# Remainder products straight from the gathered rows, two casts of ScalarE in another order, and GpSimd's lookups ahead of its first-layer product

## The chip, the cores and the metric

The kernel runs on one core of a Trainium2 chip. The metric is the device time of one execution in microseconds (us), median of three runs. Engines are called TensorE (PE in the rows), VectorE (DVE), ScalarE (ACT), GpSimd (POOL) and SyncE (SP, whose DMA queue is SPq).

## The reference

For each of 1024 samples, 32 ids look up 32 rows of 64 numbers, one in each of 32 tables. These rows are h0 (32 fields, 64 columns). Two "cross" layers follow, each a product of every pair of fields, column by column, mixed by a weight, with a bias and a relu; then a sum over the 64 columns and a small perceptron.

```
def _cin_layer(h, h0, W, b):
    Wr = W.reshape(W.shape[0], Hn, Mn)
    x = jnp.einsum('bhd,bmd,ohm->bod', h, h0, Wr) + b[None, :, None]
    return jax.nn.relu(x)
e = jnp.stack([tbl_0[ids[:, 0]], ..., tbl_31[ids[:, 31]]], axis=1)
x1 = _cin_layer(e, e, W1, b1)              # 128 outputs
x2 = _cin_layer(x1[:, :64], e, W2, b2)     # 128 outputs
z = sum over columns of concat(x1[:, 64:], x2)
h = relu(concat(z, dense_ctx) @ W_top1 + b_top1)
h = relu(h @ W_top2 + b_top2)
y = h @ W_top3
```

All is float32.

## The kernel before

**Tiling.** A chunk is 8 samples, so 8 x 64 = 512 columns; there are 128 chunks and 64 pairs of chunks. The looked-up rows of a pair come by four indirect DMAs of GpSimd (the lookups, L271) into one of three buffers `gathered`, 128 partitions (32 fields x 4) by 4 x 64 numbers. They are stored twice to a table in DRAM, `emb_rows` (L234), laid out by field. From there each chunk is loaded in several forms: `h0` (every field four times), `near` (four tiles, fields shifted by 0 to 15) and `far` (four tiles, fields shifted by 16 to 31).

**First layer.** The product of a pair of fields is symmetric, so only shifts 0 to 16 are needed. Shifts 0 to 15 are `prod1 = near * h0` (one instruction of GpSimd a chunk, L308), then eight matmuls in plain float32 (L592: four tiles, two instructions each). The shift by 16 has only 16 distinct products, field f by field f + 16: this is the remainder. Before, it is loaded from DRAM a pair of chunks at a time as `rem_a` (fields 0 to 15) and `rem_b` (fields 16 to 31), each 32 rows of 512 (L352); GpSimd multiplies them into `rem_prod` (L279), ScalarE casts the product twice to the rounded type fp32r, into two blocks of `rem_parts` (L727, L728), and GpSimd writes what the rounding lost into the third block (L295). One matmul of 96 rows (L595) adds the three blocks to the accumulator `acc1` and ends it.

**Second layer.** ScalarE takes relu and sums of `acc1` (L713, writes `x1`), SyncE replicates rows of `x1` by DMA (L251, `x1rep`), ScalarE copies that into PSUM (L762, `x1p`), and VectorE multiplies it with `near` and with `far` (L514, `pnear` and `pfar`, eight tiles each). Ten near and far tiles and three more, 13 in all, are split into a rounded part `phi` and the rest `plo`, and multiplied with rounded weights `w2hi` and `w2lo` in fp32r: two matmuls on `phi` (L604, L605) and one on `plo` (L610) for each tile. Two of these 13 tiles get their `plo` from a DMA that adds (L285, 512 KB, issued by GpSimd, in `low_parts`); the other 11 from VectorE (L519). The remaining three tiles go in plain float32 (L615, six instructions). ScalarE makes `phi` by three casts: near tiles 2 to 7 (L789), near tiles 0 and 1 (L790) and five far tiles (L801), and then takes relu and sums of the second layer's accumulator of the chunk before (L713 again, named acc<-acc).

**Order.** Each engine runs one hand-written program; they meet only in semaphores. After a fill, every engine has a function `step(c, ...)`, run for chunk c = 0 to 127. In step c TensorE does, in this order: the 12 `phi` matmuls of near tiles 2 to 7, the four of near tiles 0 and 1, the whole first layer of chunk c + 2 (L592, L595), then L615, L610 and the ten `phi` matmuls of the far tiles. ScalarE's step c begins with relu and sums of the first layer of chunk c + 1. SyncE's step c waits for these (`z1_ready`), replicates `x1`, loads `h0` and `near` of chunk c + 3, in even steps stores a pair's rows, loads `far` of chunk c + 2, and in even steps loads the remainder of the pair. GpSimd's step c does `prod1` of chunk c + 2, the adding DMA, in odd steps the remainder's product, in even steps its low part, and last two lookups; the lookups of an even step come behind a small copy of four columns of indices (L266).

TensorE's clock has two levels, 1.2 and 2.4 GHz; PEclk in the profile is the granted share of the higher.

Of the kernel before, what the change touches and what calls it, by code (L numbers as in the profile page):

```python
# [42 lines left out]
def build_dlrm(nc, a):  # L43
# [7 lines left out]
    with ctx:  # L51
# [15 lines left out]
        idx = [sb(f"idx_{s}", [P, PAIR_GATHERS], i32) for s in range(3)]  # L67
# [15 lines left out]
        rem_a = sb("rem_a", [REM, N])  # L83
        rem_b = sb("rem_b", [REM, N])
        rem_prod = sb("rem_prod", [REM, N])
        rem_parts = sb("rem_parts", [3 * REM, N], fp32r)
# [44 lines left out]
        idx_ready = sem("idx_ready")  # L131
# [20 lines left out]
        x1p_ready = sem("x1p_ready")  # L152
        rem_in = sem("rem_in")
# [101 lines left out]
        @block.gpsimd  # L255
        def _(pool):
            nc.gpsimd.memset(ident[:, :], 0.0).then_inc(ident_zero, 1)
            pool.wait_ge(ident_zero, 1)
            nc.gpsimd.affine_select(out=ident[:, :], in_=ident[:, :], compare_op=ALU.not_equal, fill=1.0,
                                    base=0, pattern=[[-1, P]], channel_multiplier=1).then_inc(ident_ready, 1)  # L260
            nc.gpsimd.memset(wt1a[0:H, :], 0.0)
            nc.gpsimd.memset(z1[0:H, :], 0.0).then_inc(top_zero, 1)
            pool.wait_ge(idx_all_ready, 1)

            def place_idx(pair, s):
                nc.gpsimd.tensor_copy(idx[s][:, :].unsqueeze(2), idx_all[:, :, bass.ds(pair, 1)]).then_inc(idx_ready, 1)  # L266
                pool.wait_ge(idx_ready, pair + 1)
                pool.sem_inc(lookups_begun, 1)

            def gather(g, s):  # L270
                nc.gpsimd.indirect_dma_start(  # L271
                    out=gathered[s][:, g, :], out_offset=None, in_=a["tables"],
                    in_offset=bass.IndirectOffsetOnAxis(ap=idx[s][:, g:g + 1], axis=0)).then_inc(rows_gathered[s], 16)

            def remainder_products(pair):
                pool.wait_ge(rem_in, 32 * pair + 32)

                pool.wait_ge(rem_lo_ready, pair)
                nc.gpsimd.tensor_tensor(rem_prod[:, :], rem_a[:, :], rem_b[:, :], ALU.mult).then_inc(rem_prod_ready, 1)  # L279

            def low_parts(c):

                pool.wait_ge(minus_ready, c + 1)
                pool.sem_inc(lo_begun, 1)
                nc.gpsimd.dma_start(plo[:, 0:T_DMA, :], pnear[:, 0, 0:T_DMA, :], accum_op=ALU.add  # L285
                                    ).then_inc(lo_dma_in, 16)

            for pair in range(3):
                place_idx(pair, pair)
                for g in range(PAIR_GATHERS):  # L290
                    gather(g, pair)

            def remainder_low(pair):
                pool.wait_ge(rem_hi_ready, pair + 1)
                nc.gpsimd.tensor_tensor(rem_parts[2 * REM:3 * REM, :], rem_prod[:, :],  # L295
                                        rem_parts[0:REM, :].bitcast(fp32), ALU.subtract).then_inc(rem_lo_ready, 1)

            def step(c, turn, u, at):
                pair, odd = turn * (U // 2) + u // 2, u % 2
                if at == 0:  # L300
                    pool.wait_ge(rem_prod_ready, 2)
                    remainder_low(1)
                    pool.wait_ge(rem_lo_ready, 2)
                if within(at, 2):

                    pool.wait_ge(acc1_ready, c + 2)
                    pool.wait_ge(near_in[(u + 2) % 3], LOADS * (turn * (U // 3)) + LOADS * ((u + 2) // 3 + 1))
                    nc.gpsimd.tensor_tensor(prod1[:, :, :], near[(u + 2) % 3][:, :, :],  # L308
                                            h0[odd][:, :].unsqueeze(1).to_broadcast([P, K1, N]), ALU.mult
                                            ).then_inc(p1_ready, 1)  # L310
# [3 lines left out]
                if not odd and begun(at) and within(at, 2):  # L314

                    pool.wait_ge(p1_ready, c + 3)
                    remainder_low(pair + 1)
                    pool.wait_ge(rem_lo_ready, pair + 2)
                if within(at, 7 - odd):
                    if not odd:  # L320
                        if at == 0:
                            pool.wait_ge(p1_ready, 3)

                        pool.wait_ge(emb_stored, STORES * pair + STORES)
                        place_idx(pair + 3, u // 2)
                    for g in range(2 * odd, 2 * odd + 2):
                        gather(g, u // 2)

            remainder_products(1)
            all_steps(step)  # L330

        @block.sync
        def _(sp):
# [28 lines left out]
            store_copy(sp, 0, 0, 0)  # L362
            sp.wait_ge(emb_stored, STORES)
            load_h0(sp, 0, 0, 0)
            load_near_tiles(sp, 0, 0, range(0, K1 // 2))
            load_rem(0)
            load_near(sp, N, 1, 1)
            store_rows(1, 1, 1)
            load_far(0, 0)
            sp.wait_ge(emb_stored, 2 * STORES)  # L370
            sp.wait_ge(rem_prod_ready, 1)
            load_rem(2 * N)
            sp.wait_ge(z1_ready, 1)
            replicate_x1(sp, [0])

# [18 lines left out]
            def step(c, turn, u, at):  # L394
# [17 lines left out]
                if not odd and within(at, 5):  # L412

                    sp.wait_ge(emb_stored, STORES * pair + 3 * STORES)
                    sp.sem_inc(stores_begun, 1)
                    sp.wait_ge(rem_prod_ready, pair + 2)
                    load_rem((c + 4) * N)
# [10 lines left out]
        def _(dve):  # L428
# [10 lines left out]
            dve.wait_ge(idx_ready, 2)  # L439
# [48 lines left out]
            def products1(s, ks):  # L488
# [7 lines left out]
            dve.wait_ge(rem_in, 32)  # L496
            nc.vector.tensor_tensor(rem_prod[:, :], rem_a[:, :], rem_b[:, :], ALU.mult).then_inc(rem_prod_ready, 1)
# [4 lines left out]
            dve.wait_ge(rem_hi_ready, 1)  # L502
            nc.vector.tensor_tensor(rem_parts[2 * REM:3 * REM, :], rem_prod[:, :],
                                    rem_parts[0:REM, :].bitcast(fp32), ALU.subtract).then_inc(rem_lo_ready, 1)
# [16 lines left out]
            def step(c, turn, u, at):  # L521
# [3 lines left out]
                if begun(at):  # L525
                    dve.wait_ge(lo_near_ready, c)
                    dve.wait_ge(lo_dma_in, 16 * c)
# [22 lines left out]
        def _(pe):  # L550
# [43 lines left out]
            def remainder1(s):  # L594
                nc.tensor.matmul(acc1[s][:, :], w1remT[:, s, :], rem_parts[:, :],  # L595
                                 start=False, stop=True).then_inc(acc1_ready, 1)

            def layer1(s):
                tiles1(s, range(K1))
                remainder1(s)  # L600
# [22 lines left out]
            pe.wait_ge(rem_lo_ready, 1)  # L623
            remainder1(0)
# [3 lines left out]
            layer1(1)  # L628
# [6 lines left out]
            def step(c, turn, u, at):  # L635
# [5 lines left out]
                pe.wait_ge(hi_dma_ready, c + 1)  # L641
                high(odd, range(0, T_DMA)).then_inc(hi_near_used, 1)
                if within(at, 2):
                    pe.wait_ge(p1_ready, c + 3)
                    pe.wait_ge(rem_lo_ready, pair + 2)
                    pe.wait_ge(z1_ready, c + 1)
                    layer1(odd)
# [5 lines left out]
                else:  # L653
# [7 lines left out]
                    top1(3)  # L661
                pe.wait_ge(pfar_ready, c + 1)
# [45 lines left out]
        def _(act):  # L708
# [16 lines left out]
            def remainder_hi(pair):  # L725
                act.wait_ge(rem_prod_ready, pair + 1)
                nc.scalar.copy(rem_parts[0:REM, :], rem_prod[:, :])  # L727
                nc.scalar.copy(rem_parts[REM:2 * REM, :], rem_prod[:, :]).then_inc(rem_hi_ready, 1)  # L728
# [15 lines left out]
            load_near_tiles(nc.scalar, 0, 0, range(K1 // 2, K1))  # L744
            act.wait_ge(w2_second, 1)
# [6 lines left out]
            remainder_hi(0)  # L752
# [20 lines left out]
            def step(c, turn, u, at):  # L773
# [6 lines left out]
                if not odd and within(at, 2):  # L780
                    remainder_hi(pair + 1)
# [8 lines left out]
                nc.scalar.copy(phi[:, 0:T_DMA, :], products[:, 0:T_DMA, :]).then_inc(hi_dma_ready, 1)  # L790
# [7 lines left out]
                act.wait_ge(pfar_ready, c + 1)  # L798
                if begun(at):
                    act.wait_ge(acc2_ready, c)  # L800
                nc.scalar.copy(phi[:, T_NEAR:T_SPLIT, :], pfar[:, :, :, :].rearrange("p a k n -> p (a k) n")[:, 0:T_SPLIT - T_NEAR, :]).then_inc(hi_far_ready, 1)  # L801
# [38 lines left out]
```

## Time and profile before

| what | value |
|---|---|
| median of three runs | 2034.03 us (2031.25 to 2035.14) |
| the profiled execution, its own time | 2035.26 us |
| span of the profile | 2033.5 us, mean granted clock 0.997 |
| TensorE busy | 1999.9 us (98%) |
| VectorE busy | 1923.5 us (95%) |
| ScalarE busy | 1713.6 us (84%) |
| GpSimd busy | 1647.3 us (81%) |
| DMA share of 16 engines, 100 to 1900 us | 0.90 to 0.91 |

Busy shares are means over the span. What sets the end is read from who waits for whom: an engine that never waits is the bound, and idle time of another costs nothing until that first one has to wait for it. Overlap of matmuls is modelled, so the distance from the start of one to the start of the next is the cost of a matmul in a stream, not its own duration.

### The profile page before, as it was taken

How to read it: one execution, taken by the hardware profiler on the slowest of the kernel's cores; microseconds unless marked ns; L12 is line 12 of the kernel's file. 1: busy time of each engine (PE TensorE's matmuls, PEld its weight loads, DVE VectorE, ACT ScalarE, POOL GpSimd, SP SyncE). 2: the span in 40 equal slices, each digit the busy share in tenths (PEclk: the TensorE clock that was granted, in tenths of full speed). 3: DMA queues.
4: the chain of work that ended last, by engine and by line, in shares of the span. 5: the costliest groups of instructions: out<-in, count | busy, mean ns of one | idle time of the engine just before them, and what ended most of it. 6: DMA issues, size and time to landing. Idle time of an engine off the chain costs nothing.

```text
span 2033.5 us, 24093 instructions
## 1 busy us (share of the span) xinstructions
PE 1999.9 (98%) x7038; PEld 1325.8 (65%) x7038; DVE 1923.5 (95%) x546; ACT 1713.6 (84%) x4887; POOL 1647.3 (81%) x708
## 2 busy tenths in 40 slices
PE   5999999999999999999999999999999999999999
PEld 3666666666666666666666666666666666666664
DVE  6999999999999999999999999999999999999991
ACT  4788888888888888888888888888888888888873
POOL 5898887879899998887889998788999988887520
PEclk9999999999999999999999999999999999999999
DMA  7898988988988989989989989989988989989950
GB/s 227 217 268 235 245 246 232 245 248 232 245 249 234 248 244 235 250 241 236 253 237 237 254 237 236 257 232 237 257 233 238 255 231 239 255 230 238 251 131 11
DMA packets 257782, 474.16 MB, mean 233 GB/s; under 512 B 35425, under 2 KB 52321, under 8 KB 257522
## 3 DMA queue, kind: packets, MB, share of 16 engines
q1 hardware_dynamic: 230450, 396.18, 64.5%
q0 software_dynamic: 26624, 75.52, 22.0%
q8 instruction: 56, 0.92, 0.2%
q10 hardware_dynamic: 576, 0.92, 0.1%
q14 instruction: 76, 0.62, 0.1%
HBM read 321.49 MB, written 16.78 MB: 166 GB/s over the span
## 4 chain that ended last, share of the span: by engine, by line
PE 90%; DMA 3%; DVE 2%; ACT 2%; issue 2%; POOL 1%; SPq 0%; DVEq 0%; POOLq 0%; ACTq 0%
PE acc L592 20%; PE acc L604 17%; PE acc L605 17%; PE acc L610 17%; PE acc L615 14%; DMA plo<-pnear 2%; DVE pnear L514 2%; PE acc L595 1%; ACT phi L789 1%; ACT x L713 1%; POOL prod L308 1%; DMA x1rep<-x 1%; PE x1p L686 0%; DMA near<-emb_rows 0%; PE acc L686 0%
## 5 line engine op out<-in xcount | busy, mean ns | idle before, releaser
L271 POOL DMA_INDIRECT gathered<-in_tables,idx x256 | 655.4, 2560 | 101.8 <-POOL idx L266 51.2
L308 POOL TENSOR_TENSOR prod<-near,h 128x2048 f32<-128x2048 f32 x126 | 582.5, 4623 | 128.5 <-PE acc L595 81.1
L604 PE MATMUL acc<-phi,w2lo 128*128 128x512 f32 x1664 | 655.2, 394 | 8.2 <-ACT phi L789 8.0
L605 PE MATMUL acc<-phi,w2hi 128*128 128x512 f32 x1664 | 654.3, 393 | 0.0
L514 DVE TENSOR_TENSOR pnear<-near,x1p 128x4096 f32<-128x4096 f32 x128 | 564.9, 4413 | 6.2 <-ACT x1p L762 3.8
L514 DVE TENSOR_TENSOR pfar<-far,x1p 128x4096 f32<-128x4096 f32 x128 | 564.9, 4413 | 0.7 <-PE acc L615 0.7
L592 PE MATMUL acc<-prod,w1T 128*128 128x512 f32 x1024 | 460.1, 592 | 1.5 <-DVE prod L489 1.5
L610 PE MATMUL acc<-plo,w2hi 128*128 128x512 f32 x1664 | 454.5, 423 | 0.0
L713 ACT ACTIVATE x<-acc,bias 128x64 f32<-128x64 f32 x1024 | 305.8, 324 | 170.6 <-PE acc L595 170.6
L519 DVE TENSOR_TENSOR plo<-pnear,phi 128x3072 fp32r<-128x3072 f32 x128 | 446.2, 3486 | 0.3 <-ACT phi L789 0.3
L519 DVE TENSOR_TENSOR plo<-pfar,phi 128x2560 fp32r<-128x2560 f32 x128 | 361.2, 2822 | 45.1 <-ACT phi L801 45.0
L610 PEld LDWEIGHTS acc<-plo,w2hi 128*128 128x128 f32 x1664 | 313.0, 188 | 120.6 <-issue 61.0
L604 PEld LDWEIGHTS acc<-phi,w2lo 128*128 128x128 f32 x1664 | 314.1, 189 | 82.3 <-ACT phi L789 12.8
L605 PEld LDWEIGHTS acc<-phi,w2hi 128*128 128x128 f32 x1664 | 314.1, 189 | 67.9
L789 ACT CAST phi<-pnear 128x3072 fp32r<-128x3072 f32 x128 | 352.7, 2756 | 0.0
L615 PE MATMUL acc<-pfar,w2T 128*128 128x512 f32 x768 | 350.6, 592 | 0.0
L592 PEld LDWEIGHTS acc<-prod,w1T 128*128 128x128 f32 x1024 | 193.6, 189 | 197.0 <-issue 184.5
L801 ACT CAST phi<-pfar 128x2560 fp32r<-128x2560 f32 x128 | 299.5, 2340 | 0.0
L713 ACT ACTIVATE acc<-acc,bias 128x64 f32<-128x64 f32 x1024 | 293.5, 291 | 4.8 <-PE acc L605 4.8
L615 PEld LDWEIGHTS acc<-pfar,w2T 128*128 128x128 f32 x768 | 145.7, 190 | 159.3 <-issue 153.7
L713 ACT ACTIVATION_READ_ACCUMULATOR x<-acc,bias 128x1 f32 x1024 | 220.9, 216 | 0.0
L713 ACT ACTIVATION_READ_ACCUMULATOR acc<-acc,bias 128x1 f32 x1024 | 218.1, 213 | 0.0
(75 smaller groups left out, 1151.3 us busy)
## 6 DMA issues: line engine op xcount, KB each, us to landing
far<-emb_rows SPq DMA_DIRECT2D x512, 256.0 KB, 4.6
near<-emb_rows SPq DMA_DIRECT2D x510, 256.0 KB
plo<-pnear POOLq DMA_DIRECT2D x128, 512.0 KB
x1rep<-x SPq DMA_DIRECT2D x255, 256.0 KB, 4.3
h<-emb_rows SPq DMA_DIRECT2D x128, 256.0 KB
emb_rows<-gathered SPq DMA_DIRECT2D x127, 128.0 KB
gathered<-in_tables,idx POOLq DMA_INDIRECT x256, 6.6
rem_a<-emb_rows SPq DMA_DIRECT2D x64, 64.0 KB
```

Of the source, the lines that this page charges most:

```text
L271: nc.gpsimd.indirect_dma_start(out=gathered[s][:, g, :], out_offset=None, in_=a["tables"], in_offset=bass.IndirectOffsetOnAxis(ap=idx[s][: ...
L308: nc.gpsimd.tensor_tensor(prod1[:, :, :], near[(u + 2) % 3][:, :, :], h0[odd][:, :].unsqueeze(1).to_broadcast([P, K1, N]), ALU.mult).then_ ...
L514: return nc.vector.tensor_tensor(out, h0part.unsqueeze(1).to_broadcast([P, A2, k, N]), x1p[s][:, :].rearrange("p (a n) -> p a n", a=A2).un ...
L519: return nc.vector.tensor_tensor(plo[:, parts, :], whole, phi[:, parts, :].bitcast(fp32), ALU.subtract)
L592: nc.tensor.matmul(acc1[s][:, :], w1T[:, k, :], prod1[:, k, :], start=(k == 0), stop=False)
L604: nc.tensor.matmul(acc2[s][:, :], w2lo[:, t, :], phi[:, t, :], start=(t == T_DMA), stop=False)
L605: mm = nc.tensor.matmul(acc2[s][:, :], w2hi[:, t, :], phi[:, t, :], start=False, stop=(t == T_SPLIT - 1))
L610: mm = nc.tensor.matmul(acc2[s][:, :], w2hi[:, t, :], plo[:, t, :], start=False, stop=False)
L615: mm = nc.tensor.matmul(acc2[s][:, :], w2T[:, k, :], pfar[:, 1, K2 - T_WHOLE + k, :], start=False, stop=False)
L713: ins = nc.scalar.activation(out[:, cols], acc[:, cols], ACT.Relu, bias=bias[:, :], accum_out=z[:, bass.ds(c * CB + b, 1)])
L789: nc.scalar.copy(phi[:, T_DMA:T_NEAR, :], products[:, T_DMA:T_NEAR, :]).then_inc(hi_near_ready, 1)
L801: nc.scalar.copy(phi[:, T_NEAR:T_SPLIT, :], pfar[:, :, :, :].rearrange("p a k n -> p (a k) n")[:, 0:T_SPLIT - T_NEAR, :]).then_inc(hi_far_ ...
```

## The change

**Remainder.** `rem_a` and the two loads from DRAM go. For each pair SyncE now moves partitions 64 to 127 of `gathered` (fields 16 to 31) to `rem_b` on partitions 0 to 63 (`move_upper`, one DMA of 64 KB), GpSimd multiplies `gathered[0:64]` with it (64 x 256 in place of 32 x 512), ScalarE makes one cast (`rem_hi`), GpSimd the low part (`rem_lo`), and SyncE places the three blocks into one of two buffers `rem_parts` by three DMAs of 64 KB (`place_remainder`). TensorE waits for these DMAs (`rem_in`, 48 a pair) ahead of the first layer, where it had waited for GpSimd's low part.

**ScalarE.** The far cast comes ahead of the copy into `x1p`, and the cast of near tiles 0 and 1 behind both. The remainder's cast moves to the end of odd steps, ahead of the second layer's relu and sums. TensorE runs the four `phi` matmuls of near tiles 0 and 1 behind the first layer, no longer ahead of it.

**GpSimd.** In each step the two lookups come first, ahead of `prod1`, and read their indices from `idx_all` directly; the copy L266 goes. The low part of the remainder comes at the head of even steps.

```diff
             def step(c, turn, u, at):        # GpSimd
                 pair, odd = turn * (U // 2) + u // 2, u % 2
-                if at == 0:
-                    pool.wait_ge(rem_prod_ready, 2)
-                    remainder_low(1)
-                    pool.wait_ge(rem_lo_ready, 2)
+                if not odd and begun(at) and within(at, 2):
+                    remainder_low(pair + 1)
+                if within(at, 7 - odd):
+                    if not odd:
+                        pool.wait_ge(emb_stored, STORES * pair + STORES)
+                        pool.wait_ge(rem_prod_ready, pair + 1)
+                    for g in range(2 * odd, 2 * odd + 2):
+                        gather(g, pair + 3, u // 2)
                 if within(at, 2):
                     pool.wait_ge(acc1_ready, c + 2)
...
                 low_parts(c)
                 if odd and within(at, 3):
-                    remainder_products(pair + 2)
...
+                    remainder_products(pair + 2, (u // 2 + 2) % 3)
...
-            def load_rem(col):
-
-                for t, f0 in ((rem_a, 0), (rem_b, HALF)):
-                    src = bass.AP(emb, f0 * ROW + col, [[ROW, HALF], [N, 2], [1, N]])
-                    sp.dma_start(t[:, :], src).then_inc(rem_in, 16)
+            def move_upper(pair, s):
+
+                if pair:
+                    sp.wait_ge(rem_prod_ready, pair)
+                sp.dma_start(rem_b[:, :, :], gathered[s][HALF * GS:F * GS, :, :]).then_inc(rem_b_in, 16)
+
+            def place_remainder(pair):
+
+                sp.wait_ge(rem_lo_ready, pair + 1)
+                if pair >= 2:
+                    sp.wait_ge(acc1_ready, 2 * pair - 2)
+                for b, part in enumerate((rem_hi, rem_hi, rem_lo)):
+                    home = rem_parts[pair % 2][b * REM:(b + 1) * REM, :].rearrange("r (w n) -> r w n", w=2)
+                    sp.dma_start(home.bitcast(fp32), part[:, :].bitcast(fp32)).then_inc(rem_in, 16)
...
                     sp.wait_ge(pnear_ready, c + 1)
                     sp.wait_ge(p1_ready, c + 2)
+                    if odd:
+                        sp.wait_ge(emb_stored, STORES * (pair + 3))
                     load_near(sp, (c + 3) * N, 1 - odd, u % 3)
+                if not odd and begun(at) and within(at, 2):
+                    place_remainder(pair + 1)
                 if not odd and within(at, 5):
                     store_rows(pair + 2, (u // 2 + 2) % 3, turn + (u // 2 + 2) // 3 + 1)
+                    move_upper(pair + 2, (u // 2 + 2) % 3)
...
                 high(odd, range(T_DMA, T_NEAR))
-                pe.wait_ge(hi_dma_ready, c + 1)
-                high(odd, range(0, T_DMA)).then_inc(hi_near_used, 1)
                 if within(at, 2):
                     pe.wait_ge(p1_ready, c + 3)
-                    pe.wait_ge(rem_lo_ready, pair + 2)
+                    pe.wait_ge(rem_in, 48 * (pair + 2))
                     pe.wait_ge(z1_ready, c + 1)
-                    layer1(odd)
+                    layer1(odd, pair + 1)
...
+                pe.wait_ge(hi_dma_ready, c + 1)
+                high(odd, range(0, T_DMA)).then_inc(hi_near_used, 1)
```

In the fill, the first remainder's product moves from VectorE to GpSimd, behind its twelve lookups, and the first layer of chunk 0 waits for its three placing DMAs.

## Rows read from the trace of the kernel before

**Rows 1.** Waits of TensorE, 100 to 1900 us: total us, times, longest

```profile
PE acc L604 <- ACT phi L789: 1.5, 3, 0.5
```

**Rows 2.** Chain that ended last, 1000 to 1034 us: start us, us

```profile
1009.53 0.23 PE acc L604
...
1012.28 0.23 PE acc L604
...
1013.20 3.43 PE acc L592 x8
...
1028.38 3.43 PE acc L592 x8
```

**Rows 3.** Timeline of ScalarE: start us, us, [idle before <- releaser]

```profile
1008.84 1.04 ACT L790 CAST phi<-pnear 128x1024 fp32r<-128x1024 f32 x1
...
1009.79 1.00 ACT L762 COPY x1p<-x1rep 128x1024 f32<-128x1024 f32 x1
...
1010.73 2.34 ACT L801 CAST phi<-pfar 128x2560 fp32r<-128x2560 f32 x1
...
1012.98 0.27 ACT L713 ACTIVATE acc<-acc,bias 128x64 f32<-128x64 f32 x1
...
1016.90 0.31 ACT L713 ACTIVATE x<-acc,bias 128x64 f32<-128x64 f32 x1 [1.47 <-PE acc L595]
...
1019.24 0.60 ACT L727 CAST rem_parts<-rem_prod 32x512 fp32r<-32x512 f32 x1
```

**Rows 4.** Timeline of SyncE's DMA queue in two even steps: issue start us, us

```profile
928.35 1.20 SPq L251 DMA_DIRECT2D x1rep<-x  x2
...
936.62 1.24 SPq L234 DMA_DIRECT2D emb_rows<-gathered  x2
...
1019.47 1.20 SPq L251 DMA_DIRECT2D x1rep<-x  x2
...
1026.56 2.57 SPq L234 DMA_DIRECT2D emb_rows<-gathered  x2
```

**Rows 5.** Timeline: a near load's issue, and the product that waits for it

```profile
900.53 5.55 SPq L242 DMA_DIRECT2D near<-emb_rows  x4
...
910.89 4.61 POOL L308 TENSOR_TENSOR prod<-near,h 128x2048 f32<-128x2048 f32 x1 [0.31 <-DMA near<-emb_rows]
```

**Rows 6.** Landing times of line L251's x1rep and L346's far loads

```profile
DMA to landing us min/median/max: 3.6/4.4/6.0
...
DMA to landing us min/median/max: 3.2/4.6/7.3
```

**Rows 7.** Timeline of TensorE behind two of its idle stretches

```profile
64.70 0.50 PE L604 MATMUL acc<-phi,w2lo 128*128 128x512 f32 x1 [2.29 <-ACT phi L789]
...
70.08 3.59 PE L592 MATMUL acc<-prod,w1T 128*128 128x512 f32 x8
...
1984.47 0.79 PE L604 MATMUL acc<-phi,w2lo 128*128 128x512 f32 x1 [4.18 <-ACT phi L789]
...
1991.05 1.02 PE L574 MATMUL acc<-z,wt1a 128*128 128x512 f32 x2
```

**Rows 8.** Busy time by window: PE PEld DVE ACT POOL, PEclk, DMA, GB/s

```profile
1986.00:1989.00 3.00, 3.00 (x9) 2.32 (x8) 3.00 (x2) 1.60 (x1) 0.00 (x0) 0.50 0.12 22
```

**Rows 9.** The page's row of the lookups: busy, mean ns, idle

```profile
L271 POOL DMA_INDIRECT gathered<-in_tables,idx x256 | 655.4, 2560 | 101.8 <-POOL idx L266 51.2
```

**Rows 10.** Chain that ended last, 0 to 100 us: the adding DMA

```profile
48.16 8.21 DMA plo<-pnear
```

**Rows 11.** Timeline of VectorE and GpSimd in steady state

```profile
1015.88 4.41 DVE L514 TENSOR_TENSOR pnear<-near,x1p 128x4096 f32<-128x4096 f32 x1
...
1022.91 0.99 POOL L285 DMA_DIRECT2D plo<-pnear  x1
```

**Rows 12.** Timeline of the fill: GpSimd's last lookup, TensorE's first remainder

```profile
25.38 1.42 POOL L271 DMA_INDIRECT gathered<-in_tables,idx  x1 [0.30 <-issue]
...
28.89 0.80 PE L595 MATMUL acc<-rem_parts,w1remT 96*128 96x512 f32 x1
```

More of the change, by code:

```diff
@@ L66, in build_dlrm @@
         idx_all = sb("idx_all", [P, PAIR_GATHERS, PAIRS], i32)
-        idx = [sb(f"idx_{s}", [P, PAIR_GATHERS], i32) for s in range(3)]
         gathered = [sb(f"gathered_{s}", [P, PAIR_GATHERS, D]) for s in range(3)]
@@ L82, in build_dlrm @@
         far = [sb(f"far_{s}", [P, K2, N]) for s in range(2)]
[L83 to L86, printed above, removed]
+        rem_b = sb("rem_b", [HALF * GS, PAIR_GATHERS, D])
+        rem_prod = sb("rem_prod", [HALF * GS, PAIR_GATHERS * D])
+        rem_hi = sb("rem_hi", [HALF * GS, PAIR_GATHERS * D], fp32r)
+        rem_lo = sb("rem_lo", [HALF * GS, PAIR_GATHERS * D], fp32r)
+        rem_parts = [sb(f"rem_parts_{s}", [3 * REM, N], fp32r) for s in range(2)]
         prod1 = sb("prod1", [P, K1, N])
@@ L152, in build_dlrm @@
         x1p_ready = sem("x1p_ready")
+        rem_b_in = sem("rem_b_in")
         rem_in = sem("rem_in")
@@ L312, in step @@
                 if odd and within(at, 3):
-                    remainder_products(pair + 2)
[L314 to L329, printed above, removed]
+                    remainder_products(pair + 2, (u // 2 + 2) % 3)
+            for pair in range(2):
+                remainder_products(pair, pair)
+                remainder_low(pair)
             all_steps(step)
@@ L362, in _ @@
             store_copy(sp, 0, 0, 0)
+            move_upper(0, 0)
             sp.wait_ge(emb_stored, STORES)
@@ L365, in _ @@
             load_near_tiles(sp, 0, 0, range(0, K1 // 2))
-            load_rem(0)
             load_near(sp, N, 1, 1)
             store_rows(1, 1, 1)
+            move_upper(1, 1)
+            place_remainder(0)
             load_far(0, 0)
             sp.wait_ge(emb_stored, 2 * STORES)
-            sp.wait_ge(rem_prod_ready, 1)
-            load_rem(2 * N)
             sp.wait_ge(z1_ready, 1)
             replicate_x1(sp, [0])
+            place_remainder(1)
             sp.wait_ge(tp_copied, 2)
@@ L411, in step @@
                     load_far((c + 2) * N, odd)
[L412 to L417, printed above, removed]
                 if at == 3:
@@ L592, in tiles1, with remainder1, layer1 @@
                     nc.tensor.matmul(acc1[s][:, :], w1T[:, k, :], prod1[:, k, :], start=(k == 0), stop=False)
-            def remainder1(s):
-                nc.tensor.matmul(acc1[s][:, :], w1remT[:, s, :], rem_parts[:, :],
+            def remainder1(s, pair):
+                nc.tensor.matmul(acc1[s][:, :], w1remT[:, s, :], rem_parts[pair % 2][:, :],
                                  start=False, stop=True).then_inc(acc1_ready, 1)
-            def layer1(s):
+            def layer1(s, pair):
                 tiles1(s, range(K1))
-                remainder1(s)
+                remainder1(s, pair)
             def high(s, parts):
@@ L622, in _ @@
             tiles1(0, range(K1 // 2, K1))
-            pe.wait_ge(rem_lo_ready, 1)
-            remainder1(0)
+            pe.wait_ge(rem_in, 48)
+            remainder1(0, 0)
             turn(6, *NEAR_TURNS[1])
@@ L726, in remainder_hi @@
                 act.wait_ge(rem_prod_ready, pair + 1)
-                nc.scalar.copy(rem_parts[0:REM, :], rem_prod[:, :])
-                nc.scalar.copy(rem_parts[REM:2 * REM, :], rem_prod[:, :]).then_inc(rem_hi_ready, 1)
+                if pair:
+                    act.wait_ge(rem_in, 48 * pair)
+                nc.scalar.copy(rem_hi[:, :], rem_prod[:, :]).then_inc(rem_hi_ready, 1)
             act.wait_ge(ident_ready, 1)
@@ L779, in step @@
                     layer1(c + 1, 1 - odd)
-                if not odd and within(at, 2):
-                    remainder_hi(pair + 1)
                 act.wait_ge(pnear_ready, c + 1)
@@ L789, in step @@
                 nc.scalar.copy(phi[:, T_DMA:T_NEAR, :], products[:, T_DMA:T_NEAR, :]).then_inc(hi_near_ready, 1)
-                nc.scalar.copy(phi[:, 0:T_DMA, :], products[:, 0:T_DMA, :]).then_inc(hi_dma_ready, 1)
+                act.wait_ge(pfar_ready, c + 1)
+                if begun(at):
+                    act.wait_ge(acc2_ready, c)
+                nc.scalar.copy(phi[:, T_NEAR:T_SPLIT, :], pfar[:, :, :, :].rearrange("p a k n -> p (a k) n")[:, 0:T_SPLIT - T_NEAR, :]).then_inc(hi_far_ready, 1)
                 if within(at, 1):
@@ L797, in step @@
                     copy_x1rep(1 - odd)
[L798 to L801, printed above, removed]
+                nc.scalar.copy(phi[:, 0:T_DMA, :], products[:, 0:T_DMA, :]).then_inc(hi_dma_ready, 1)
+                if odd and within(at, 3):
+                    remainder_hi(pair + 2)
                 if at == CHUNKS - 1:
```

40 lines of the change are left out of this document (17 added, 23 removed).

## The prediction

> **What bounds the kernel now.** I read the page first, but busy shares don't decide here: four engines are above 80%. The view that decides is TensorE's list of waits. From 100 to 1900 us it waited 1.5 us in all [rows 1]. The chain that ended last says the same: step after step it is TensorE's matmuls end to end, and the first layer of one chunk starts 15.18 us behind that of the chunk before [rows 2]. So the steady part is 15.2 us of matmuls a step and no wait. The change leaves every matmul in place. It can win nothing there; it can win in the fill and the drain, which are few, or it can lose wherever something that TensorE waits for now comes too late. The reader should therefore ask of each edit only this: when is it ready, and when does TensorE want it?
>
> I count from s, the start of TensorE's step c with c odd, 1009.53 in the rows. In the kernel before the first layer begins at s + 3.67, behind sixteen phi matmuls; the thirteenth of them starts at 1012.28, s + 2.75 [rows 2]. Its end shows in ScalarE, which waited for it and began relu and sums at 1016.90, s + 7.37 [rows 3]; SyncE could replicate x1 at 1019.47, 2.57 us later [rows 3, 4]. That is the even step's SyncE program, and the change adds to it.
>
> **The remainder's new way (the term that decides).** In even steps SyncE places the pair's three blocks behind its near load, and TensorE wants them ahead of the first layer of the same even step. Before, this had a step of slack: the loads were SyncE's last work and the low part was GpSimd's. Now both ends lie in one step, so I add up the way between.
>
> - The first layer now stands behind twelve matmuls, so the wanted time in the even step is s + 15.18 + 2.75 = s + 17.93, and the odd step's first layer ends at s + 2.75 + 3.66 = s + 6.4 (3.43 and a remainder of 0.23).
> - ScalarE begins its far cast at s at the earliest, since it needs the accumulation that ends there. By distances from start to start: far cast 2.25, copy into x1p 0.94, near cast 0.95 [rows 3]. The remainder's cast of 64 x 256 does half the columns of one that took 0.60 [rows 3]; I take 0.3, with nothing and 0.6 as ends. Then relu and sums of the second layer; eight pairs like it, from the row of 1016.90 to the cast behind them at 1019.24, take 2.3 [rows 3]. Sum 6.8, so ScalarE is free at about s + 6.9, past s + 6.4. The relu of the first layer starts there, 0.5 us sooner than before.
> - SyncE's replication: + 2.57, at s + 9.5.
> - From the replication to the end of the near load (where the stores now start): 1019.47 to 1026.56 is 7.1 us, 928.35 to 936.62 is 8.3 [rows 4]. I take 7.9: place_remainder begins at s + 17.4 (16.6 to 17.8). It is already about the time at which TensorE wants the data.
> - Three DMAs; one issue costs 0.6 by the pair of replications (1.20 for two) [rows 4], so the third starts 1.25 us on, at s + 18.6.
> - Landing. No row shows 64 KB behind a near load. The nearest are 256 KB ones: 4.4 in the median and 3.6 at least for x1rep, which copies inside SBUF too, 4.6 (3.2 to 7.3) for far [rows 6]. The last near load itself landed at 910.89, 4.8 us behind the end of its issue at 906.08 [rows 5]. I take 4.4, the same kind of copy; ends 3.2 and 7.3. Landed at s + 23.0 (21.0 to 26.4).
>
> TensorE waits from s + 17.93 to s + 23.0: **5.1 us a pair** (3.1 to 8.5). By the Trainium skill (DMA: Bandwidth & Descriptors, Anatomy of one DMA) one DMA costs about 2.0 us and its bytes by 436 GB/s, 2.15 us for 64 KB; the wait would be 2.8 us by that, an estimate by that page. The rows here have 3.6 at the least for 256 KB, where that rule gives 2.6, so I stay with the rows.
>
> **The clock behind the wait.** After 2.29 us idle the sixteen phi matmuls took from 64.70 to 70.08, 5.4 us, and after 4.18 us idle from 1984.47 to 1991.05, 6.6 us [rows 7]; in steady state they take 3.67 [rows 2]. The granted clock behind the second was 0.50 [rows 8], the lower of the two levels. So an idle stretch costs another 1.7 to 2.9 us. Mine is 5.1 long: I take 2.8, ends 0 and 3.
>
> The odd step gets nothing back, because TensorE is full of its own work from there. The relation of every other engine eases (VectorE's 1923.5 us over 128 steps is 15.0 a step, against a mean of 19). A pair costs 7.9 us more. Places happen in even steps 2 to 124, 62 of them: 62 x 7.9 = 490 us.
>
> **ScalarE's order.** What VectorE waits for the far cast goes when the far cast comes first. It is worth nothing, since TensorE waits for nobody. The near cast of tiles 0 and 1 ends at s + 4.1, wanted behind the first layer at s + 6.4: hidden. If that cover were gone, its 0.95 would fall on TensorE. The copy into x1p is 1.3 us later than before, at s + 2.3 to 3.3; VectorE wants it at s + 6.35 (1015.88) [rows 11]: hidden. TensorE frees near tiles 0 and 1 3.7 us later, at s + 7.3; ScalarE touches them again behind 10 us: hidden.
>
> **GpSimd's order.** Dropping L266 frees one copy and its idle, 0.8 us each (51.2 us in all) [rows 9]. Against that the low part now waits for ScalarE's cast at the end of the odd step, s + 4.5, and with it the two lookups, prod1 and the adding DMA queued behind. Low part 0.7 (half of a 32 x 512 one's work; estimate from the 0.60 cast, ends 0.3 and 1.3), lookups 2 x 2.56 and 0.3 of issue each, prod1 4.6 [rows 5, 9]: prod1 ends at s + 15.6, wanted at s + 17.93: hidden. The adding DMA starts at s + 15.6; before it was s + 13.4 (1022.91) [rows 11]. Landed 8.2 us later [rows 10], at s + 23.8, where VectorE wanted to overwrite pnear at about 1015.88 + 15.18, s + 21.5. That 2.3 us lie inside the wait above. If that wait is not there, this one is (a rival below).
>
> **Fill.** The first remainder was done at 28.89 [rows 12]. Now GpSimd starts it behind twelve lookups, which ended at 26.80 [rows 12], about 24 without the copies. Product 0.7, cast 0.3, low part 0.7, issue 1.85, landing 4.4: about 32. I count 4 us of loss (0 to 8). Two or three moves of 64 KB more a pair are below 3% of the DMA's bytes: 0.
>
> **Sum.** 2035.3 (the profiled execution's own time, 1.2 us over the median of the runs) + 490 + 4 = 2529. The slower pace leaves the DMA engines emptier, so near loads are issued nearer to 7.1 than 7.9; that takes off about 0.3 a pair, 19 us. I forecast **2510 us**.
>
> **Rivals.**
> A. The wait is there but shorter: near issue 7.1, landing 3.2, 3.1 us a pair, and with a clock loss of 1.7 it is 4.8 x 62: 2035 + 298 = 2333; with no fall of the clock 2230. For: emptier DMA engines. Against: rows 7 show the fall after 2.29 us.
> B. The blocks land in time, by a shorter issue than any row has. Then the adding DMA decides: 2.3 late, less the 0.7 that ScalarE's phi now has in hand (pnear 4.4 and casts 3.8 from s + 21.5 end at s + 29.7, wanted at s + 30.4): 1.6 x 62, 2134 us. It decides once the place is under s + 18.
> C. Much longer: landing 7.3 behind near's backlog, 8.5 + 3 a pair, 2035 + 713 = 2750.
> D. Faster: everything lands in time and TensorE stays full. Then only the fill counts: three index copies of about 1 us less, and of the idle in [rows 7] 2.29 us: some 5 us, 2030. Its point is a landing before s + 17.93, so a place of three DMAs within 0.5 us of its begin. No row is near. The same edits with the fill's loss against them give no change, 2034.
>
> **How the numbers follow.** Forecast (2400 to 2650) 0.60; A 0.20; B 0.08; C 0.05; D 0.04; no change 0.03. The range leaves out most of B, D and the top of C: 2220 to 2670. A run of this kernel repeats within about 0.2%, so that is the bound of no change. Faster 0.04, same 0.03, slower 0.93.
>
> **What would show it.** The list of waits of TensorE must have L592 behind the DMA of rem_parts, about 62 times, 4 to 6 us each; granted clock about 0.5 for some 5 us behind each; SyncE's three placing issues about 17 us behind s; VectorE and GpSimd's shares down to about 77% and 66%. If TensorE's waits name phi or plo, B is right. I would be wrong if SyncE got through its near load in 4 us, or if the data were wanted a step later than I read the counts.

## The result and the profile after

The changed kernel takes 2500.86 us (median of four runs, 2497.16 to 2508.85) against 2034.34 us. The ratio is 1.230, 95% interval 1.227 to 1.234: slower by 467 us, or 7.52 us for each of the 62 pairs of chunks that are placed in the loop. The forecast was 2510 us.

The page of the changed kernel, span, engines, clock and DMA share:

```profile
span 2507.0 us, 24032 instructions
...
PE 2134.1 (85%) x7038; PEld 1366.7 (55%) x7038; DVE 1916.3 (76%) x544; ACT 1663.8 (66%) x4823; POOL 1223.2 (49%) x646
...
PEclk9989999899889889899999898899999899999999
DMA  7777678778777677687787787777777777777760
```

No engine has more work that would explain it: VectorE, ScalarE and GpSimd are all busy for less time than before. The list of waits of TensorE, 100 to 2400 us, is what answers to [rows 1]:

```profile
PE acc L591 <- issue: 329.6, 60, 6.6
```

There was one reason to wait in the steady part, worth 1.5 us; now there is another, ahead of the first layer (L591), once a pair, 5.5 us each. Over the whole execution it is 339.8 us in 62 waits. The profile can't name the releaser here and says "issue". TensorE waits for three things in that place: prod1, the blocks (`rem_in`) and x1's relu (`z1_ready`). Which of them it is, the experiments must tell. The page's row of these matmuls shows the second part of the loss:

```profile
L591 PE MATMUL acc<-prod,w1T 128*128 128x512 f32 x1024 | 587.2, 727 | 341.3 <-issue 339.8
```

The same 1024 matmuls were busy for 460.1 us before (592 ns each). So 127.1 us went into their being slower. 339.8 + 127.1 = 466.9 of the 473.5 us between the two spans. The other 6.6 us are a sum of small parts: TensorE starts the remainder matmul of chunk 3 3.2 us later than before (76.31 against 73.11), the drain behind the last one is 3.5 us shorter (69.8 against 73.3), and some 7 us lie in the steady part, outside these two rows.

The chain that ended last, over one pair (answers to [rows 2]):

```profile
1028.03 0.23 PE acc L603
...
1030.77 3.43 PE acc L591 x8
...
1045.97 5.19 issue
1051.17 5.88 PE acc L591 x8
```

An odd step c starts at s = 1028.03. Its first layer takes 3.43 us at once. In the even step behind it the first layer was due at 1045.97 and starts 5.19 us later, and then takes 5.88 us for the same eight matmuls. One pair earlier the wait was 6.57 us, up to 1012.64, and the eight took 6.37 us. The windows around that earlier first layer (columns as in [rows 8]) show the clock at the lower level, and back at 0.99 in the third window:

```profile
1012.00:1015.00 3.00, 2.36 (x3) 1.18 (x4) 2.17 (x1) 0.00 (x0) 0.00 (x0) 0.50 0.92 293
1015.00:1018.00 3.00, 3.00 (x5) 1.12 (x4) 0.00 (x0) 0.00 (x0) 0.00 (x0) 0.50 0.03 12
1018.00:1021.00 3.00, 3.00 (x11) 1.82 (x10) 0.00 (x0) 1.72 (x12) 1.67 (x1) 0.99 0.00 0
```

What TensorE waited for stands in the timeline of SyncE's queue in the same even step (answers to [rows 4]):

```profile
1037.43 1.20 SPq L253 DMA_DIRECT2D x1rep<-x  x2
1038.73 1.15 SPq L239 DMA_DIRECT2D h<-emb_rows  x1
1039.92 4.63 SPq L244 DMA_DIRECT2D near<-emb_rows  x4
1044.65 2.48 SPq L354 DMA_DIRECT2D rem_parts<-rem_hi  x2
1047.17 0.61 SPq L354 DMA_DIRECT2D rem_parts<-rem_lo  x1
```

The first placing DMA is issued 1.3 us ahead of the time at which TensorE wants all three landed, and the third 1.2 us behind it.

### The profile page after: what moved, and what is told of

It is laid out like the page before. It is cut to its first block, busy times and chain, and to the rows that moved or that the text cites. A ratio compares the mean times of both kernels' runs of the same rounds, so it can differ in the third digit from the quotient of the medians.

```text
span 2507.0 us, 24032 instructions
## 1 busy us (share of the span) xinstructions
PE 2134.1 (85%) x7038; PEld 1366.7 (55%) x7038; DVE 1916.3 (76%) x544; ACT 1663.8 (66%) x4823; POOL 1223.2 (49%) x646
## 4 chain that ended last, share of the span: by engine, by line
PE 83%; issue 14%; DVE 1%; DMA 0%; ACT 0%; SPq 0%; POOL 0%; DVEq 0%; POOLq 0%; ACTq 0%
PE acc L591 23%; PE acc L603 15%; PE acc L604 15%; PE acc L609 15%; PE acc L614 13%; PE acc L594 1%; DVE pnear L512 0%; DMA plo<-pnear 0%; PE x1p L685 0%; PE acc L685 0%; ACT phi L789 0%; DVE plo L517 0%; DMA near<-emb_rows 0%; POOL prod L313 0%; PE x1p L562 0%
## 5 line engine op out<-in xcount | busy, mean ns | idle before, releaser
L512 DVE TENSOR_TENSOR pfar<-far,x1p 128x4096 f32<-128x4096 f32 x128 | 565.9, 4421 | 509.7 <-PE acc L614 509.7
L591 PE MATMUL acc<-prod,w1T 128*128 128x512 f32 x1024 | 587.2, 727 | 341.3 <-issue 339.8
L512 DVE TENSOR_TENSOR pnear<-near,x1p 128x4096 f32<-128x4096 f32 x128 | 565.4, 4417 | 19.4 <-DMA plo<-pnear 13.9
L591 PEld LDWEIGHTS acc<-prod,w1T 128*128 128x128 f32 x1024 | 236.3, 238 | 629.5 <-issue 622.5
L517 DVE TENSOR_TENSOR plo<-pnear,phi 128x3072 fp32r<-128x3072 f32 x128 | 431.9, 3374 | 0.0
L268 POOL DMA_INDIRECT gathered<-in_tables,idx_all x256 | 392.3, 1532 | 71.5 <-issue 66.2
L517 DVE TENSOR_TENSOR plo<-pfar,phi 128x2560 fp32r<-128x2560 f32 x128 | 361.5, 2824 | 0.0
L712 ACT ACTIVATE acc<-acc,bias 128x64 f32<-128x64 f32 x1024 | 287.5, 284 | 5.7 <-PE acc L604 5.7
L788 ACT ACTIVATE plo<-pnear 128x1024 fp32r<-128x1024 f32 x128 | 136.1, 1063 | 184.3 <-PE acc L609 171.4
L295 POOL TENSOR_TENSOR rem_lo<-rem_prod,rem_hi 64x256 fp32r<-64x256 f32 x64 | 75.6, 1181 | 369.2 <-ACT rem_hi L729 368.7
L712 ACT ACTIVATION_READ_ACCUMULATOR x<-acc,bias 128x1 f32 x1024 | 228.5, 223 | 0.0
```

Of the source, the lines that this page charges most:

```text
L268: nc.gpsimd.indirect_dma_start(out=gathered[s][:, g, :], out_offset=None, in_=a["tables"], in_offset=bass.IndirectOffsetOnAxis(ap=idx_all[ ...
L512: return nc.vector.tensor_tensor(out, h0part.unsqueeze(1).to_broadcast([P, A2, k, N]), x1p[s][:, :].rearrange("p (a n) -> p a n", a=A2).un ...
L517: return nc.vector.tensor_tensor(plo[:, parts, :], whole, phi[:, parts, :].bitcast(fp32), ALU.subtract)
L591: nc.tensor.matmul(acc1[s][:, :], w1T[:, k, :], prod1[:, k, :], start=(k == 0), stop=False)
L712: ins = nc.scalar.activation(out[:, cols], acc[:, cols], ACT.Relu, bias=bias[:, :], accum_out=z[:, bass.ds(c * CB + b, 1)])
```

## The experiments

All ratios are to the kernel before, timed on the same chip. Each kernel's own first layer is L591 unless a row says otherwise.

### The blocks ahead of the near load

```diff
                     replicate_x1(sp, range(A2))
+                if not odd and begun(at) and within(at, 2):
+                    place_remainder(pair + 1)
                 if within(at, 3):
...
                     load_near(sp, (c + 3) * N, 1 - odd, u % 3)
-                if not odd and begun(at) and within(at, 2):
-                    place_remainder(pair + 1)
```

> The changed kernel with the three placing DMAs issued behind the replication of x1 and ahead of the near load, in the same even step. Theory (TensorE waits for the placing DMAs because they stand behind the near load on SyncE's queue): they are issued 5 to 6 us sooner, land at about s + 16 to 17, ahead of s + 17.93, and TensorE's wait ahead of the first layer goes. What is left is the later adding DMA, some 1.6 us a pair at the most: 2040 to 2140 us. Rival (the wait has another cause, such as x1's relu, prod1 or the semaphore of the rows): the time stays at 2450 to 2510 us.

Measured: 2120.9 us, ratio 1.041 (1.037 to 1.045). 82% of the loss is gone by an exchange of two calls. The size is inside what I gave, but not for the reason given: I had expected the wait at the first layer to go and the adding DMA to cost what is left. TensorE's waits, 100 to 2000 us:

```profile
PE acc L591 <- issue: 71.0, 51, 1.9
```

It still waits at the first layer, 1.4 us a pair, and 62 x 1.4 is the 86 us. In one pair the third placing DMA was issued at 1035.15 and the first layer began at 1041.08, 5.9 us later (5.5 in the mean of the 62 pairs), where I had counted on 4.4. The blocks now stand between the replication and the near load; that sharing the DMA engines with these two is what makes the landing longer is likely and not shown. That prod1 (done at 1034.5) and x1's relu (1030.9) were long ready leaves only the blocks; this is an argument by elimination.

### The blocks at the head of the step

```diff
+                if not odd and begun(at) and within(at, 2):
+                    place_remainder(pair + 1)
                 if within(at, 1):
                     sp.wait_ge(z1_ready, c + 2)
```

and the call behind the near load is taken out, as above.

> The changed kernel with the three placing DMAs at the head of SyncE's even step, ahead of its wait for x1's relu. The low part is ready by then, so they fall into SyncE's idle time and delay no load. Theory: TensorE's wait for the blocks goes and near is not delayed, so that only the later adding DMA of even steps can cost: 2035 to 2134 us. If it costs nothing the time is that of the kernel before less what the fill gives, 2030 to 2040 us. Rival (three small DMAs more a pair are dear by themselves wherever they stand): over 2200 us.

Measured: 2035.63 us, ratio 1.0006 (0.9996 to 1.0016). The whole loss of 466 us is gone. The same three DMAs, bytes, casts and lookups cost next to nothing in the steady part when the DMAs stand in SyncE's idle time ahead of its wait for x1: from the remainder matmul of chunk 3 to that of chunk 127 it is 1888.0 us, against 1887.0 before. That the totals are equal is partly luck: the fill is 5.6 us longer (chunk 3's remainder matmul starts at 78.75, before at 73.11) and the drain 3.5 us shorter. TensorE's waits are down to 4.3 us from 100 to 2000 us, and none is at the first layer. VectorE does now wait for the adding DMA, as the second rival had it:

```profile
DVE pnear L512 <- DMA plo<-pnear: 33.9, 41, 2.2
```

0.8 us each and 2.2 at the most; but TensorE doesn't wait for VectorE in turn. That rival's mechanism is there and its price was wrong.

### The blocks still later

The call stands behind the stores, the move of the upper half and the far load.

```diff
                     load_far((c + 2) * N, odd)
+                if not odd and begun(at) and within(at, 2):
+                    place_remainder(pair + 1)
```

> The changed kernel with the three placing DMAs still later, behind the stores, the move of the upper half and the far load, 4.4 us further down SyncE's even step. Theory (the place on the queue sets the wait one for one): 62 x 4.4 = 270 us more, 2770 us (2700 to 2840). Rival (only the near load's backlog mattered, which has drained by then, or the wait is for another thing): 2500 to 2600 us.

Measured: 2789.43 us, ratio 1.371 (1.369 to 1.373). All 62 waits of the execution:

```profile
PE acc L591 <- issue: 604.8, 62, 11.1
```

9.75 us each against 5.48, so 4.3 more. Over the 62 pairs the third placing DMA is issued 4.6 us later behind the replication than in the changed kernel, and the first layer begins 4.05 us behind that issue where it was 4.34: 4.6 - 0.3 is the 4.3. The time rose by 288.6 us, 4.65 a pair. Four places on one queue, four times: 2035.6, 2120.9, 2500.9, 2789.4 us.

### Tiles first, then the wait

```diff
-                    pe.wait_ge(rem_in, 48 * (pair + 2))
                     pe.wait_ge(z1_ready, c + 1)
-                    layer1(odd, pair + 1)
+                    tiles1(odd, range(K1))
+                    pe.wait_ge(rem_in, 48 * (pair + 2))
+                    remainder1(odd, pair + 1)
```

> The changed kernel with the wait for the placing DMAs moved from ahead of the first layer's eight matmuls to ahead of the one remainder matmul, 3.43 us later in TensorE's stream. Theory: the blocks arrive when they did, so the wait shrinks from 5.2 to 6.6 us to 1.8 to 3.2 us a pair, with the clock's loss at 0 to 1.9 us: 62 x (2.5 + 1.5) over 2034 is 2280 us (2150 to 2350). Rival (prod1 or x1's relu are what is late, since they are waited for in the same place as before): no change, 2500 us.

Measured: 2221.86 us, ratio 1.092 (1.089 to 1.094). Only the wait for the blocks was moved, and the profile now names it (TensorE's waits, whole execution):

```profile
PE acc L594 <- DMA rem_parts<-rem_lo: 125.7, 62, 3.2
```

2.03 us a pair against 5.48, 3.45 less: the 3.43 us of eight matmuls that now run under it. The time fell by 4.50 a pair; the 1.05 left over is what the shorter idle stretch gives back by the clock, as I read it (mean granted clock 0.975, against 0.93 in the changed kernel).

### No idle ahead of the wait

```diff
-                    pe.wait_ge(rem_in, 48 * (pair + 2))
                     pe.wait_ge(z1_ready, c + 1)
+                    if not odd and begun(at):
+                        for _ in range(6):
+                            nc.tensor.matmul(acc1[odd][:, :], w1T[:, 0, :], flat(w1T[:, 0:N // O, :]), start=True, stop=True)
+                    pe.wait_ge(rem_in, 48 * (pair + 2))
                     layer1(odd, pair + 1)
```

> The changed kernel with twelve spare matmuls (5.2 us at the full clock) ahead of the wait for the placing DMAs in even steps, written to the accumulator that the first layer then clears; all other work is the same. They add work and change nothing of the result. Theory (each wait costs a second time because the clock falls behind it): the blocks arrive when they did, the clock stays up and the 2.4 to 2.9 us that the eight matmuls took more go: 2500 - 62 x 2.7 = 2330 us (2310 to 2400). Rival (the clock's loss is not on the path, or the spare matmuls add to it): 2500 us or more.

Measured: 2389.14 us, ratio 1.175 (1.172 to 1.177). TensorE does more work and the kernel is 111.7 us faster. The timeline of TensorE shows the spare matmuls, and then the eight at full clock:

```profile
1030.16 5.31 PE L645 MATMUL acc<-w1T 128*128 128x512 f32 x12
1035.83 3.70 PE L591 MATMUL acc<-prod,w1T 128*128 128x512 f32 x8 [0.36 <-DMA rem_parts<-rem_lo]
```

The spare matmuls stand behind the waits for prod1 and for x1's relu. They follow the phi matmuls at once, in the whole execution TensorE never waits ahead of them (its list of waits has no L645), and the wait behind them is now put down to the blocks. So neither prod1 nor the relu is late at the first layer, and what the first experiment left to elimination is shown here. The clock's part, too, was on the path. It is 111.7 / 62 = 1.80 us a pair, not the 2.7 that I had read from two pairs. The spare work and what is left of the wait cost (2389.1 - 2034.7) / 62 = 5.7 us a pair: the wait without its clock.

### The casts alone

The kernel before with ScalarE's new order of casts, TensorE's four matmuls of near tiles 0 and 1 behind the first layer, and VectorE's wait `hi_dma_ready`.

```diff
                 high(odd, range(T_DMA, T_NEAR))
-                pe.wait_ge(hi_dma_ready, c + 1)
-                high(odd, range(0, T_DMA)).then_inc(hi_near_used, 1)
...
+                pe.wait_ge(hi_dma_ready, c + 1)
+                high(odd, range(0, T_DMA)).then_inc(hi_near_used, 1)
                 pe.wait_ge(pfar_ready, c + 1)
```

> The kernel before with one part of the change alone: ScalarE's far cast ahead of the copy into x1p, the cast of near tiles 0 and 1 behind both, TensorE's four matmuls of these tiles behind the first layer, and VectorE's wait for that cast. Theory (hidden, TensorE stays full in the steady part): 2030 to 2040 us; what moves is the drain. Rival (the copy into x1p, now 1.3 us later, or the late release of near tiles 0 and 1 holds VectorE and through it phi): TensorE waits for phi in most steps, over 2060 us.

Measured: 2027.56 us, ratio 0.9968 (0.9956 to 0.9981). This part makes the kernel 6.6 us faster, which I had put at nothing; it lies below my 2030 to 2040. TensorE waits nowhere between 100 and 1900 us. The two traced executions are 8.1 us apart, and the gain stands in three places. In the fill it is 2.3 us by the remainder matmul of chunk 3 (70.80 against 73.11): TensorE stood still for 1.40 us there and its clock stayed up, where it had been 2.29 us with a slow clock behind it [rows 7]. In the steady part it is 2.2 us, with the three waits of [rows 1] gone. In the drain it is 3.5 us. Where TensorE stood still for 4.18 us and then ran on a slow clock [rows 7], it now waits twice (1900 us to the end)

```profile
PE acc L605 <- ACT phi L802: 1.7, 1, 1.7
...
PE acc L605 <- ACT phi L790: 0.5, 1, 0.5
```

and the granted clock behind both is 1.00. VectorE no longer waits for the far cast (41.4 us in 85 waits before, 100 to 1900 us), so it runs ahead as far as TensorE lets it. That is worth 0.8 us: its last pnear starts 15.36 us behind TensorE's last remainder matmul (1970.96 and 1955.60), and before 16.15 (1976.27 and 1960.12). The larger part of the 3.5 us is that the idle time comes in two short pieces and the clock doesn't fall.

### The lookups alone

The kernel before with the two lookups at the head of GpSimd's step, indices straight from `idx_all`, and no copy L266.

```diff
+                if within(at, 7 - odd):
+                    if not odd:
+                        pool.wait_ge(emb_stored, STORES * pair + STORES)
+                    for g in range(2 * odd, 2 * odd + 2):
+                        gather(g, pair + 3, u // 2)
                 if within(at, 2):
                     pool.wait_ge(acc1_ready, c + 2)
```

> The kernel before with another part alone: GpSimd's two lookups at the head of each step and with indices straight from the whole array, no copy of indices; the remainder stays as it was. Theory: GpSimd's cyclic order is nearly the same, TensorE waits for none of it: 2030 to 2040 us. Rival (lookups ahead of the first-layer product make prod1 or the adding DMA late): over 2050 us.

Measured: 2040.48 us, ratio 1.0033 (1.0021 to 1.0045). This part costs 6 us, just outside what I gave. TensorE's waits in the steady part are 2.2 us. In the traced execution, 4.5 us longer than that of the kernel before, the remainder matmul of chunk 3 is 4.1 us late (77.20 against 73.11), the steady part adds 1.6 and the drain takes 1.2 off: it is mostly the fill. Which wait of the fill is not split further.

### Best of the parts

The kernel with the blocks at the head, with four edits of the fill:

```diff
+                if at == 0:
+                    low_parts(c)
                 if within(at, 2):
...
             replicate_x1(sp, [0])
-            place_remainder(1)
...
             load_near(sp, 2 * N, 0, 2)
+            place_remainder(1)
...
             last.then_inc(near_staged, 1)
+            remainder_hi(0)
...
-                pool.sem_inc(lookups_begun, 1)
+                if pair == 0:
+                    nc.gpsimd.memset(mark[:, :], 0.0).then_inc(lookups_begun, 1)
```

> The kernel with the placing DMAs at the head of SyncE's even steps, and four edits of its fill: the second placing behind the near load of chunk 2 and not ahead of it, the first adding DMA ahead of prod1 of chunk 2, ScalarE's first remainder cast behind its copies of weights, and VectorE's weight work held back until GpSimd has really done the first four lookups. Theory (its drain is already some 5 us shorter than in the kernel before and its fill longer by as much): 2026 to 2032 us, under the kernel before by 0.2% or so. Rival (the fill is bound elsewhere): 2034 to 2037 us.

Measured: 2028.9 us, ratio 0.9974 (0.9963 to 0.9984). The change with its blocks in the right place and its fill mended beats the kernel before by 5.3 us. It doesn't beat the casts alone (2027.56 us), so no run shows a gain by the remainder's new way or by GpSimd's new order. The four edits of the fill were not timed one by one.

The casts alone, with the first adding DMA ahead of prod1 of chunk 2:

```diff
                     pool.wait_ge(rem_lo_ready, 2)
+                    low_parts(c)
                 if within(at, 2):
```

> The kernel before with the casts' part of the change and one more edit: GpSimd issues the first adding DMA ahead of prod1 of chunk 2, some 4 us sooner. Theory (VectorE's second pnear waited 2.3 us for that DMA, TensorE for the phi made from it, and its clock fell behind it): 2.3 us of wait and some 1.5 us of slow matmuls less than the casts alone, 2021 to 2025 us. Rival (prod1 of chunk 2, now 1 us later, takes its place): 2026 to 2030 us.

Measured: 2027.48 us, ratio 0.9962 (0.9949 to 0.9976), which is what the casts alone give. The second pnear came only 0.35 us sooner (56.34, against 56.69 there) and not 1.8. Two timelines of VectorE, first with the casts alone, then with the edit, show why:

```profile
48.12 4.08 DVE L519 TENSOR_TENSOR plo<-pnear,phi 128x3072 fp32r<-128x3072 f32 x1
...
56.69 4.42 DVE L514 TENSOR_TENSOR pnear<-near,x1p 128x4096 f32<-128x4096 f32 x1 [1.76 <-DMA plo<-pnear]
```

```profile
47.31 6.36 DVE L521 TENSOR_TENSOR plo<-pnear,phi 128x3072 fp32r<-128x3072 f32 x1
...
56.34 4.41 DVE L516 TENSOR_TENSOR pnear<-near,x1p 128x4096 f32<-128x4096 f32 x1
```

The wait for the DMA is gone, but GpSimd's prod1, now at 45.86 to 50.46, lies beside VectorE's subtraction, which takes 6.36 us in place of 4.08 (more on this at the end). The time is inside what I gave for the rival, which was also prod1, but for another reason.

## Why the prediction was right, step by step

**The bound.** Right. TensorE was full and each edit was worth only what it made TensorE wait.

**The way of the remainder.** Right at nearly every station. With s = 1028.03:

| station | forecast | measured |
|---|---|---|
| relu and sums of x1 begin | s + 6.9 | 1034.88, s + 6.9 |
| replication of x1 | s + 9.5 | 1037.43, s + 9.4 |
| place_remainder begins | s + 17.4 | 1044.65, s + 16.6 |
| third placing DMA | s + 18.6 | 1047.17, s + 19.1 |
| blocks wanted | s + 17.93 | 1045.97, s + 17.9 |
| blocks landed, first layer begins | s + 23.0 | 1051.17, s + 23.1 |

Two errors partly cancel. From the replication to the first placing DMA it is 7.3 us in the mean of the 62 pairs, where I had 7.9: the near load was issued faster. From the first placing DMA to the third it is 2.4 us, where I had 1.25; behind the far load and at the head of the step it was 1.3, right behind the replication 2.9. Why an issue of the same 64 KB takes longer in some places is not shown. The landing was 4.0 us behind the third issue here and 5.6 us one pair earlier (1007.09 to 1012.64), 4.34 in the mean; I had taken 4.4. Over all pairs the wait is 5.48 us; forecast 5.1, less 0.3 for emptier DMA engines. That the blocks set it is shown by their move both ways, by the spare matmuls, and by their name in the profile once only they were waited for in that place. The list of waits of the changed kernel itself says "issue" where I had forecast their name. By the Trainium skill (DMA: Bandwidth & Descriptors, Anatomy of one DMA) a DMA of 64 KB is about 2.15 us, an estimate by its fit; that section is on DMAs which GpSimd issues, and these are SyncE's, a difference that the prediction passes over. The shortest of the 62 landings behind a near load is 3.5 us here, and the measurement decides.

**The clock.** The mechanism is right, the term of 2.8 us too large. The eight matmuls lost 127.1 / 62 = 2.05 us a pair, and taking the idle away gave 1.80. It happens in every pair: from the first of the eight to the remainder matmul it is 3.03 us before, and 4.5 to 6.2 us in each of the 62 pairs. I had used the longer of two idle stretches [rows 7] as the rule for waits of this length. The Trainium skill (TensorE: Matmul & The Clock Gate, HAM oscillation) describes such a case: a wait for a DMA in every round throttles the engine in every round. The trace agrees: granted clock 0.50 behind the wait.

**The sum.** 5.48 + 2.05 = 7.53 a pair against 7.9 and 0.3 off it, 7.6. The wait was 0.7 too small, the clock 0.75 too large. The total came out within 10 us because they cancel, which is luck; the range had to carry both.

**ScalarE's order** was costed at nothing and gives 6.6 us, in the fill, in three short waits and in the drain. I had looked at the steady part only, and had both idle stretches, 2.29 and 4.18 us, among my own rows [rows 7]. One reading was off too: the copy into x1p moves from s + 0.3 to s + 2.3, so by 2.0 us and not 1.3. It stays hidden, since VectorE wants it at s + 6.35.

**GpSimd's order** was hidden, as forecast, but by other numbers. The timeline of GpSimd in the changed kernel, from the end of the odd step:

```profile
1032.73 1.18 POOL L295 TENSOR_TENSOR rem_lo<-rem_prod,rem_hi 64x256 fp32r<-64x256 f32 x1 [5.95 <-ACT rem_hi L729]
1034.08 1.06 POOL L268 DMA_INDIRECT gathered<-in_tables,idx_all  x1 [0.16 <-issue]
1035.43 0.96 POOL L268 DMA_INDIRECT gathered<-in_tables,idx_all  x1 [0.30 <-issue]
1036.40 4.62 POOL L313 TENSOR_TENSOR prod<-near,h 128x2048 f32<-128x2048 f32 x1
```

The wait for ScalarE's cast is there (s + 4.7), but the two lookups took 1.0 us each, not 2.56 [rows 9], so the adding DMA started at 1040.97, s + 12.9 and not s + 15.6. With the blocks at the head it started at s + 13.8 (1030.52), VectorE was ready for the overwrite at 1037.54 and waited 0.8 us, where I had counted 2.3. That is why the second rival, some 1.6 us a pair, doesn't bite when the blocks are out of the way. For the same reason GpSimd's share came out at 49% and not at 66%: its lookups took 392.3 us in all, and before 655.4. VectorE's 76% is as forecast.

**The fill.** I had said 4 us of loss. The first layer of chunk 0 ended at 35.0 us against 29.7, 5.3 more; by chunk 3 it was 3.2. The drain, which the sum left out, gave 3.5 us back, so that the two together are about nothing.

## What to carry to other kernels

When an engine is full, an edit is worth the time by which its result is early or late there, so add up the way of each moved thing in the frame of that engine's step: wanted at, ready at. A small DMA placed behind a large load on one queue is issued only when the load's own issues are through; look for the queue's idle stretch, here ahead of a wait, and put it there. And read the fill and the drain as well as the steady part: an order that is worth nothing in every step may shorten the few waits that are there, and with them what the clock takes behind them.

## What the runs showed of the hardware

GpSimd's lookups cost by what VectorE does when they begin. In the kernel with the blocks at the head, one lookup stands beside VectorE's subtraction of two operands in SBUF (L517) and one beside its product with an operand in PSUM (L512):

```profile
1000.99 3.35 DVE L517 TENSOR_TENSOR plo<-pnear,phi 128x3072 fp32r<-128x3072 f32 x1
...
1001.40 3.88 POOL L268 DMA_INDIRECT gathered<-in_tables,idx_all  x1 [0.30 <-issue]
...
1022.79 4.41 DVE L512 TENSOR_TENSOR pnear<-near,x1p 128x4096 f32<-128x4096 f32 x1
...
1023.62 1.06 POOL L268 DMA_INDIRECT gathered<-in_tables,idx_all  x1 [0.15 <-issue]
```

3.88 us against 1.06 for the same instruction. This is no general slowing: the lookup stands still until the subtraction is over. In the kernel before, 184 of the 256 lookups began inside a subtraction of VectorE, and every one of them ended 0.84 to 0.94 us behind that subtraction's end. It goes the other way too. The first subtraction of `pnear` and `phi` is the only one that overlaps prod1, by 0.87 us in the kernel before, 2.26 in the changed one and 3.15 in the last experiment; it took 4.09, 5.48 and 6.36 us. Time less overlap is 3.22 us each time, against 3.35 us for the subtraction undisturbed: for as long as the prod1 that began first still runs, the subtraction makes next to no progress. The Trainium skill (GPSIMD Engine Reference, Key points) says that GpSimd shares its SBUF interfaces with VectorE and contends with instructions of two SBUF inputs; these rows agree and give the size. Over the changed kernel the mean lookup is 1532 ns, against 2560 before [rows 9], because only 68 of them now begin inside a subtraction.
